# Input weights of a state-space convolution: a product by a weighing matrix, or transposes of a weighed table

## The chip, the cores and the metric

The kernel runs on one core of one Trainium2 chip. The metric is the device time of one execution in microseconds (us): 608.1 as the median of three runs of the kernel before (607.81 to 609.33).

The engines are TensorE (PE, with its weight loads as PEld), VectorE (DVE), ScalarE (ACT), GpSimd (POOL) and SyncE (SP), which only issues transfers. Each works through its own list of instructions in order; semaphores hold an instruction until what it reads is there.

## The reference

```python
# x: (128, 64, 1024) fp32 = batch, head, position; length: (128,) ints
A = -exp(log_A_real) + 1j*A_imag;  dtA = A * exp(log_dt)[:, None]       # 64 heads x 64 states
Cs = C * (exp(dtA) - 1) / A
K  = 2 * einsum('hn,hnl->hl', Cs, exp(dtA[:, :, None] * arange(L))).real
u  = x * (arange(L) < length)                # mask
y  = causal_conv(u, K) + u * D               # the FFT of length 2L is this convolution
y  = y * mask
logits = y @ route_w.T;  w = one_hot(argmax) * max                      # 8 experts
out = x + ((w x (y @ A.T)) @ Bw)             # rank 16 per expert
```

The recurrence is linear, so the convolution of 1024 positions is done in four stretches of Q = 256: inside a stretch by a Toeplitz matrix of K, and from stretch to stretch by the 64 complex states (128 real rows), which are carried with exp(256 dtA).

## The kernel before, in words

A batch of 128 lies on the partitions, and the 64 heads are worked through one after the other, in a software pipeline: step i (line 311, `run_steps`) does some stages for head i, others for heads i-1, i+1, i+2 and i+3. The order on every engine is the order in which the code of that engine is written: a prologue for the first heads by hand, and then its `step` function 64 times. There is no scheduler. Semaphores named for what is done (`grev_done`, `b_mm`, ...) count heads.

For one head the stages are:
- Tables. Every four heads (a `Part`), GpSimd makes step tables (`angle_steps`, L446), ScalarE scales them to turns (L575, L577), VectorE rounds them (`whole_turns`, L867), GpSimd subtracts (`turn_parts`, L457), VectorE finishes and clamps the fraction (L875, L882), ScalarE takes the sine (L583), GpSimd weighs with the magnitudes (`weigh`, L465) and ScalarE mirrors halves (L597). Then per head GpSimd forms `both` (L473) and adds its halves to `Grev` (L483), the powers exp(dtA l) for l = 255..0, states on partitions. `Ghi` and `Glo` (L604, L490) are its split in two parts of lower precision, whose three products give full precision.
- Inputs: how much each of the 256 positions of a stretch gives to each state. TensorE multiplies Grev by the 128x129 matrix `Mx` (L1128, `inputs`): its 128 columns weigh and mix the real and imaginary rows, and the last gives the kernel K itself. ScalarE builds Mx from the constant `twin` and table columns (`m_matrix`, L611, L613). The result `psB` lies in the bank psO0, which the last stage (`up`) also uses. ScalarE and VectorE split it into `Bhi` and `Blo` (L623, L953); the K column goes by `kcol`, a VectorE transpose `krow` (L947) and DRAM, from where it comes back skewed as the Toeplitz table `Traw` (L340, L348), and is split into `Thi` (ScalarE, L629) and `Tlo` (GpSimd, L497).
- Bring (`psS`, L1078): six products of Bhi/Blo and Xhi/Xlo give the states that each stretch brings. ScalarE copies the first (L652), VectorE carries on to the others (`carry`, L936, L940), ScalarE and GpSimd split them (`Shi` L657, `Slo` L512).
- `turn_x`: eight transposes of x (psXe, psXo, L1092); then Xhi (L635), xeven (L640), Xlo (L889 and L505).
- `within` and `from_states` (psYe, psYo, L1078): 9 and 6 products; VectorE masks (`cut`, L966) to Y.
- `project` (psZ, L1103): eight full-precision products give logits and y @ A.T; five short VectorE instructions find the expert and gate (L902 to L924); `turn_wh` transposes (L1162); `whi`, `wlo` (L662, L959); `up` (psO) six products with Bw; VectorE adds x (L975) and the result is stored.

TensorE's order in step i is: bring(i), turn_x(i+1), inputs(i+2), project(i-1), within(i), turn_wh(i-1), from_states(i), up(i-1).

## Time and profile before

| | |
|---|---|
| median of 3 runs | 608.1 us (607.81 to 609.33) |
| profiled execution | 608.38 us, span 606.6 us, granted TensorE clock 0.995 |
| PE busy | 585.7 us, 97% of the span |
| PEld | 532.4 us, 88% |
| DVE | 489.4 us, 81% |
| POOL | 384.1 us, 63% |
| ACT | 315.8 us, 52% |
| chain that ended last | PE 91%, DVE 3%, others 1% or less |

A busy share is a mean over the whole span. Which engine sets the pace is read from the timeline of a stretch: an engine whose instructions follow one another without a hole. In a timeline row the first number is the start, the second the time of all instructions that the row groups; on TensorE a product's duration overlaps the next one's start, so what a group costs is the distance from its start to the next group's start. A full-precision fp32 product is recorded as more than one pass (x4 for two products), a transpose as one.

### The profile page before, as it was taken

Reading aid. Unit: us, or ns where it says so; the run is one execution under the profiler, and the core shown is the slowest. Engines: PE = TensorE matmul, PEld = TensorE weight load, DVE = VectorE, ACT = ScalarE, POOL = GpSimd, SP = SyncE. Lnnn points to the kernel's source line nnn. Section 1 sums busy time; section 2 is a strip of 40 time slices with the busy share of each in tenths; the row PEclk is TensorE's granted clock in tenths of the full one; section 3 lists DMA queues with packets and bytes.
Section 4 is the critical chain, followed back from the end, with each engine's and each line's share of the span. In section 5 each row is a group of like instructions: output and inputs, shape, how many; then the busy total and the mean of one; then the engine's idle time right before and its main releaser. Section 6 shows DMA issues by size and latency. Waiting matters only on the chain.

```text
span 606.6 us, 13395 instructions
## 1 busy us (share of the span) xinstructions
PE 585.7 (97%) x3657; PEld 532.4 (88%) x3657; DVE 489.4 (81%) x1369; ACT 315.8 (52%) x1060; POOL 384.1 (63%) x519
## 2 busy tenths in 40 slices
PE   3879999999999999999999999999999999999996
PEld 3868899999999999999999999999999999999994
DVE  7859878788887878888787888878788887878874
ACT  4747565556446455644645564464556456445420
POOL 4578856666685666667566666756666675675430
PEclk9999999999999999999999999999999999999998
DMA  7114344345334434544443453444345344435521
GB/s 140 54 53 115 130 149 147 103 144 157 112 132 150 147 102 144 158 105 138 150 146 103 145 157 105 138 151 142 107 145 157 101 141 152 134 112 148 157 79 70
DMA packets 37584, 77.65 MB, mean 128 GB/s; under 512 B 12477, under 2 KB 20863, under 8 KB 37511
## 3 DMA queue, kind: packets, MB, share of 16 engines
q1 hardware_dynamic: 28358, 43.76, 28.8%
q10 hardware_dynamic: 9152, 33.03, 13.3%
q8 instruction: 32, 0.52, 0.3%
q14 instruction: 42, 0.34, 0.2%
HBM read 43.16 MB, written 33.62 MB: 127 GB/s over the span
## 4 chain that ended last, share of the span: by engine, by line
PE 91%; DVE 3%; issue 1%; DMA 1%; ACT 1%; ACTq 0%; DVEq 0%; SPq 0%
PE psYo L1078 19%; PE psZ L1103 19%; PE psO L1078 15%; PE psYe L1078 13%; PE psS L1078 11%; PE psO L1128 5%; PE psXo L1092 4%; PE psXe L1092 4%; PE psZ L1162 1%; DVE psS L936 1%; DMA Traw<-kdram 1%; DVE ost L975 0%; DMA kdram<-krow 0%; DVE Sf L940 0%; DVE rho L295 0%
## 5 line engine op out<-in xcount | busy, mean ns | idle before, releaser
L512 POOL TENSOR_TENSOR Slo<-Sf,Shi 128x384 fp32r<-128x384 f32 x64 | 65.2, 1019 | 169.0 <-ACT Shi L657 169.0
L1103 PE MATMUL psZ<-Wt,Y 128*128 128x136 f32 x1024 | 129.2, 279 | 0.0
L936 DVE SCALAR_TENSOR_TENSOR psS<-Sf,tab,psS 64x128 f32<-64x128 f32 x256 | 91.8, 359 | 45.4 <-ACT Sf L652 38.5
L1103 PEld LDWEIGHTS psZ<-Wt,Y 128*128 128x128 f32 x1024 | 123.3, 190 | 0.1
L652 ACT ACTIVATE Sf<-psS 128x128 f32<-128x128 f32 x64 | 17.8, 278 | 198.8 <-PE psS L1078 198.8
L975 DVE TENSOR_TENSOR ost<-psO,xt 128x512 f32<-128x512 f32 x128 | 88.0, 690 | 2.2 <-PE psO L1078 2.0
L505 POOL TENSOR_TENSOR Xlo<-xeven,Xhi 128x512 fp32r<-128x512 f32 x63 | 81.4, 1292 | 0.0
L473 POOL TENSOR_TENSOR both<-coarse,fine 128x512 f32<-128x512 f32 x64 | 68.0, 1063 | 3.4 <-ACT fine L597 3.2
L959 DVE TENSOR_TENSOR wlo<-psZ,whi 128x128 fp32r<-128x128 f32 x64 | 18.7, 292 | 45.1 <-ACT whi L662 45.1
L1078 PE MATMUL psO<-Bw_hi,whi 128*128 128x512 f32 x128 | 50.7, 396 | 3.4 <-ACT whi L662 3.4
L1078 PE MATMUL psO<-Bw_hi,wlo 128*128 128x512 f32 x128 | 51.1, 399 | 0.0
L1078 PE MATMUL psO<-Bw_lo,whi 128*128 128x512 f32 x128 | 50.8, 397 | 0.0
L1078 PE MATMUL psYo<-Xhi,Thi 128*128 128x512 f32 x128 | 50.7, 396 | 0.0
L1078 PE MATMUL psYo<-Xlo,Thi 128*128 128x512 f32 x128 | 50.6, 396 | 0.0
L1078 PE MATMUL psYo<-Xhi,Tlo 128*128 128x512 f32 x128 | 50.3, 393 | 0.0
L483 POOL TENSOR_TENSOR Grev<-both 128x256 f32<-128x256 f32 x64 | 46.8, 732 | 5.0
L490 POOL TENSOR_TENSOR Glo<-Grev,Ghi 128x256 fp32r<-128x256 f32 x64 | 48.1, 751 | 0.7 <-ACT Ghi L604 0.7
L940 DVE SCALAR_TENSOR_TENSOR Sf<-Sf,tab,psS 128x128 f32<-128x128 f32 x128 | 44.5, 348 | 4.5
L497 POOL TENSOR_TENSOR Tlo<-Traw,Thi 128x256 fp32r<-128x256 f32 x64 | 47.1, 735 | 0.2
L657 ACT ACTIVATE Shi<-Sf 128x384 fp32r<-128x384 f32 x64 | 33.7, 526 | 25.5 <-DVE Sf L940 25.5
L1092 PE MATMUL psXe<-ident,xt 128*128 128x128 f32 x256 | 38.8, 274 | 6.9 <-DMA xt<-in_x_dram 6.9
L966 DVE TENSOR_TENSOR Y<-psYe,mask 128x512 f32<-128x512 f32 x64 | 44.1, 689 | 0.8 <-PE psYe L1078 0.8
(200 smaller groups left out, 1526.5 us busy)
## 6 DMA issues: line engine op xcount, KB each, us to landing
xt<-in_x_dram SPq DMA_DIRECT2D x64, 512.0 KB, 4.8
out_dram<-ost ACTq DMA_DIRECT2D x63, 512.0 KB, 5.1
Traw<-kdram SPq DMA_DIRECT2D x64, 128.0 KB, 2.9
kdram<-krow SPq DMA_DIRECT2D x64, 1.0 KB
A_nat<-in_L_ffn_A_dram SPq DMA_DIRECT2D x1, 512.0 KB, 5.0
B_nat<-in_L_ffn_Bw_dram SPq DMA_DIRECT2D x8, 64.0 KB, 3.5
out_dram<-ost SPq DMA_DIRECT2D x2, 256.0 KB, 2.0
lens_i<-in_itok_B_dram SPq DMA_DIRECT2D x1, 64.0 KB, 4.9
```

What stands on the lines that cost most here:

```text
L473: pool.tensor_tensor(both[:, :, :, :], coarse[:, :, h.n, :].rearrange("p t (a b) -> p t a b", b=1).to_broadcast(wide), fine[:, :, h.n, :]. ...
L483: pool.tensor_tensor(Grev[h.s2][:, :], both[:, 0, :, :].rearrange("p a b -> p (a b)"), both[:, 1, :, :].rearrange("p a b -> p (a b)"), ALU ...
L490: pool.tensor_tensor(Glo[h.s4][:, :], Grev[h.s2][:, ::-1], Ghi[h.s4][:, :].bitcast(F32), ALU.subtract).then_inc(glo_done, 1)
L497: pool.tensor_tensor(Tlo[h.s2][:, :, :].rearrange("p a b -> p (a b)"), Traw[h.s2][:, ::-1], Thi[h.s2][:, :, :].rearrange("p a b -> p (a b) ...
L505: pool.tensor_tensor(Xlo[h.s2][:, 0, :], xeven[:, :], Xhi[h.s2][:, 0, :].bitcast(F32), ALU.subtract).then_inc(xlo_even, 1)
L512: pool.tensor_tensor(Slo[h.s2][:, :], Sf[h.s2][:, :], Shi[h.s2][:, :].bitcast(F32), ALU.subtract).then_inc(slo_done, 1)
L936: dve.scalar_tensor_tensor(psS[to, new], Sf[h.s2][fr, old], tab2[fr, BR, h.n:h.n + 1], psS[to, new], ALU.mult, ALU.add).then_inc(brought_d ...
L940: dve.scalar_tensor_tensor(Sf[h.s2][:, new], Sf[h.s2][:, old], col(tab2[:, LR, :], h), psS[:, new], ALU.mult, ALU.add).then_inc(s_carried, 1)
L975: dve.tensor_tensor(ost[h.s2][:, half], psO[j][:, :], xt[h.s4][:, half], ALU.add).then_inc(added, 1)
L1078: mm = pe.matmul(dst, a, b, start=first and i == 0, stop=last and i == n - 1, skip_group_check=True)
L1092: last = pe.transpose(psX[j][:, c * P:(c + 1) * P], xt[h.s4][:, at:at + P], ident[:, :])
L1103: last = pe.matmul(psZ[:, 0:NW], Y[:, j, c, :], Wt[:, 2 * c + j, :], start=(j == 0 and c == 0), stop=(j == 1 and c == NE - 1), skip_group_ ...
```

## The change

The input weights are the same numbers, made in another way. GpSimd and ScalarE weigh the table Grev elementwise while it lies with states on the partitions: `cross_parts` (two copies that swap the halves and scale by table column MB), `same_part` (a copy scaled by MA), `w_table` (the GpSimd sum `Wg`). TensorE then only transposes the two halves of Wg to psB. K comes from the same table: the copies that read psB sum 64 columns each into `kcol` (`accum_out`), and K at position 0, with D added, is computed once for all heads in the prologue (`K0`, which takes the place of CK in pack2), so that kcol has three columns and the two zero rows in DRAM, the matrix `twin` and `Dcol` go. For head 0 VectorE makes Wg (`first_w_table`).

The order changes too: the input transposes stand behind the projection, VectorE does the five gate instructions ahead of x_lo, ScalarE does w_hi ahead of turns and mirror and x_even ahead of Shi, the inputs, krow and Blo of head 2 move from the first step into the prologue, and the magnitudes of heads 8 to 63 (rho16, Exp) are made in two portions of 16 and 40 heads instead of one of 56.

```diff
+        RHO_PARTS = [(0, 2 * FIRST), (2 * FIRST, 4 * FIRST), (6 * FIRST, H - 6 * FIRST)]
 # SyncE
-                sp.dma_start(bass.AP(kdram.tensor, h.s2 * (P + Q), [[G32, P // G32], [P, 2], [1, G32]]),
+                sp.dma_start(bass.AP(kdram.tensor, h.s2 * (P + Q), [[G32, P // G32], [P, 3], [1, G32]]),
...
-            for s in range(2):
-                sp.dma_start(kdram[s:s + 1, Q:Q + P], zeros[:, :]).then_inc(pad_done, 16)
 # GpSimd
+            def w_table(h):
+                need(pool, crossed, h.n * 2 + 2)
+                need(pool, same_done, h.n)
+                need(pool, b_mm, h.n - 1)
+                pool.tensor_tensor(Wg[h.s2][:, :], same[:, :], cross[:, :], ALU.add).then_inc(wg_done, 1)
...
                 if head(3).there and not is_head(head(0), 1):
                     g_table(head(3))
+                if head(2).there:
+                    w_table(head(2))
                 if head(0).there:
                     s_lo(head(0))
 # ScalarE
-            def m_matrix(h):
-                need(act, b_mm, h.n - 1)
-                for j, table in enumerate((M0, M1)):
-                    act.activation(Mx[h.s2][:, j * N:(j + 1) * N], twin[:, j * N:(j + 1) * N], ACT.Copy,
-                                   scale=col(tab2[:, table, :], h)).then_inc(mx_done, 1)
-                act.activation(Mx[h.s2][:, P:P + 1], col(tab2[:, CK, :], h), ACT.Copy).then_inc(mx_done, 1)
+            def cross_parts(h):
+                need(act, grev_done, h.n + 1)
+                need(act, wg_done, h.n)
+                for to, fr in ((slice(0, N), slice(N, P)), (slice(N, P), slice(0, N))):
+                    act.activation(cross[to, :], Grev[h.s2][fr, :], ACT.Copy,
+                                   scale=tab2[fr, MB, h.n:h.n + 1]).then_inc(crossed, 1)
+            def same_part(h):
+                act.activation(same[:, :], Grev[h.s2][:, :], ACT.Copy,
+                               scale=col(tab2[:, MA, :], h)).then_inc(same_done, 1)
             def b_hi(h):
-                act.activation(kcol[h.s2][:, 0, 0:1], psB[:, 0, P:P + 1], ACT.Copy).then_inc(kcol_done, 1)
-                act.activation(kcol[h.s2][:, 1, 0:1], psB[:, 1, P:P + 1], ACT.Identity,
-                               bias=Dcol[:, h.n:h.n + 1]).then_inc(kcol_done, 1)
+                for j in range(2):
+                    act.activation(scrap[:, j, :], psB[:, j, 0:N], ACT.Copy,
+                                   accum_out=kcol[h.s2][:, j, 0:1]).then_inc(kcol_done, 1)
+                act.activation(kcol[h.s2][:, 2, 0:1], col(tab2[:, K0, :], h), ACT.Copy).then_inc(kcol_done, 1)
...
             def step(head):
+                if head(2).there:
+                    cross_parts(head(2))
+                    same_part(head(2))
                 if head(-2).there:
                     store(head(-2))
                 if head(0).there:
                     first_state(head(0))
-                if head(3).there:
-                    m_matrix(head(3))
 # VectorE
+            def first_w_table(h):
+                need(dve, crossed, h.n * 2 + 2)
+                dve.scalar_tensor_tensor(Wg[h.s2][:, :], Grev[h.s2][:, :], col(tab2[:, MA, :], h), cross[:, :],
+                                         ALU.mult, ALU.add).then_inc(wg_done, 1)
...
+            link(dve.reduce_sum(ksum[:, :], CK[:, 0, :], axis=AX.X))
+            TT(pack2[:, K0, 0, 0:1], ksum[:, :], D_nat[:, :], ALU.add).then_inc(pack2_done, 1)
 # TensorE
-                need(pe, mx_done, h.n * 3 + 3)
-                need(pe, grev_done, h.n + 1)
+                need(pe, wg_done, h.n + 1)
                 for j in range(2):
-                    last = pe.matmul(psB[:, j, :], Grev[h.s2][:, j * P:(j + 1) * P],
-                                     Mx[h.s2][:, :], start=True, stop=True, skip_group_check=True)
+                    last = pe.transpose(psB[:, j, :], Wg[h.s2][:, j * P:(j + 1) * P], ident[:, :])
...
-                if is_head(head(0), 1):
-                    inputs(head(1))
-                elif head(2).there:
-                    inputs(head(2))
                 if head(-1).there:
                     project(head(-1))
-                if is_head(head(0), 1):
+                if head(2).there:
                     inputs(head(2))
```

On TensorE, in a step of the middle of the program, the end of bring and the start of within stood so before:

```order
L1078 MATMUL psS<-Xhi,Blo 128x384
L1092 MATMUL psXe<-ident,xt 128x128 x4
L1092 MATMUL psXo<-ident,xt 128x128 x4
L1128 MATMUL psO<-Mx,Grev 128x129 x2
L1103 MATMUL psZ<-Wt,Y 128x136 x8
L1078 MATMUL psYe<-Xhi,Thi 128x512
```

and stand so now, in the same step:

```order
L1101 MATMUL psS<-Xhi,Blo 128x384
L1115 MATMUL psXe<-ident,xt 128x128 x4
L1115 MATMUL psXo<-ident,xt 128x128 x4
L1126 MATMUL psZ<-Wt,Y 128x136 x8
L1150 MATMUL psO<-ident,Wg 128x128 x2
L1101 MATMUL psYe<-Xhi,Thi 128x512
```

The two products of 129 columns became two transposes and moved behind the eight products of the projection.

On GpSimd, where a step's extra work (`angle_steps` and `weigh`) comes, it stood so before, from the end of one step to the Slo of the next:

```order
L490 TENSOR_TENSOR Glo<-Grev,Ghi 128x256
L446 TENSOR_TENSOR step_h<-tab,grid 128x64
L446 TENSOR_TENSOR step_t<-tab,grid 128x64
L446 TENSOR_TENSOR step_l<-tab,grid 128x64
L465 TENSOR_TENSOR coarse<-wave,mag 128x64
L465 TENSOR_TENSOR fine<-wave,mag 128x64 x2
L473 TENSOR_TENSOR both<-coarse,fine 128x512
L483 TENSOR_TENSOR Grev<-both 128x256
L512 TENSOR_TENSOR Slo<-Sf,Shi 128x384
```

and now:

```order
L488 TENSOR_TENSOR Glo<-Grev,Ghi 128x256
L435 TENSOR_TENSOR step_h<-tab,grid 128x64
L435 TENSOR_TENSOR step_t<-tab,grid 128x64
L435 TENSOR_TENSOR step_l<-tab,grid 128x64
L454 TENSOR_TENSOR coarse<-wave,mag 128x64
L454 TENSOR_TENSOR fine<-wave,mag 128x64 x2
L462 TENSOR_TENSOR both<-coarse,fine 128x512
L474 TENSOR_TENSOR Grev<-both 128x256
L482 TENSOR_TENSOR Wg<-same,cross 128x256
L510 TENSOR_TENSOR Slo<-Sf,Shi 128x384
```

One instruction came in: the sum Wg, behind all of the step's table work and ahead of Slo.

On ScalarE the start of a step stood so before:

```order
L652 ACTIVATE Sf<-psS 128x128
L611 ACTIVATE Mx<-twin,tab 128x64 x2
L613 ACTIVATE Mx<-tab 128x1
L635 ACTIVATE Xhi<-psXe 128x512
L635 ACTIVATE Xhi<-psXo 128x512
L619 ACTIVATE kcol<-psO 128x1
L620 ACTIVATE kcol<-psO,Dcol 128x1
L623 ACTIVATE Bhi<-psO 128x256
L657 ACTIVATE Shi<-Sf 128x384
L640 ACTIVATE xeven<-psXe 128x512
```

and now:

```order
L617 ACTIVATE cross<-Grev,tab 64x256 x2
L622 ACTIVATE same<-Grev,tab 128x256
L657 DMA out_dram<-ost 128x1024
L664 ACTIVATE Sf<-psS 128x128
L647 ACTIVATE Xhi<-psXe 128x512
L647 ACTIVATE Xhi<-psXo 128x512
L652 ACTIVATE xeven<-psXe 128x512
L669 ACTIVATE Shi<-Sf 128x384
L631 ACTIVATE scrap,kcol<-psO 128x64 x2
L633 ACTIVATE kcol<-tab 128x1
L635 ACTIVATE Bhi<-psO 128x256
```

The weighing copies stand ahead of the first state, and everything that reads psB stands behind Shi.

## Rows read from the trace of the kernel before

**Rows 1.** Timeline, TensorE, head 31: start us, us, engine line operation.
```profile
304.86 0.34 PE L1078 MATMUL psS<-Xhi,Bhi 128*128 128x384 f32 x1
...
305.91 0.60 PE L1092 MATMUL psXe<-ident,xt 128*128 128x128 f32 x4
...
306.34 0.60 PE L1092 MATMUL psXo<-ident,xt 128*128 128x128 f32 x4
...
306.78 0.61 PE L1128 MATMUL psO<-Mx,Grev 128*128 128x129 f32 x4
...
307.22 2.02 PE L1103 MATMUL psZ<-Wt,Y 128*128 128x136 f32 x16
...
308.99 0.48 PE L1078 MATMUL psYe<-Xhi,Thi 128*128 128x512 f32 x1
...
313.72 0.34 PE L1078 MATMUL psS<-Xhi,Bhi 128*128 128x384 f32 x1
```

**Rows 2.** Costliest groups: busy us, mean ns, then idle before, and its releaser.
```profile
L652 ACT ACTIVATE Sf<-psS 128x128 f32<-128x128 f32 x64 | 17.8, 278 | 198.8 <-PE psS L1078 198.8
...
L959 DVE TENSOR_TENSOR wlo<-psZ,whi 128x128 fp32r<-128x128 f32 x64 | 18.7, 292 | 45.1 <-ACT whi L662 45.1
```

**Rows 3.** Timeline, GpSimd, heads 31 and 32, with the extra work.
```profile
309.60 1.01 POOL L512 TENSOR_TENSOR Slo<-Sf,Shi 128x384 fp32r<-128x384 f32 x1 [3.45 <-ACT Shi L657]
...
314.81 1.05 POOL L473 TENSOR_TENSOR both<-coarse,fine 128x512 f32<-128x512 f32 x1
315.94 0.73 POOL L483 TENSOR_TENSOR Grev<-both 128x256 f32<-128x256 f32 x1
```

**Rows 4.** Groups by form, ScalarE: a copy of 256 columns and one of 1.
```profile
L604 ACT ACTIVATE Ghi<-Grev 128x256 fp32r<-128x256 f32 x64 | 26.1, 408 | 3.7 <-POOL Grev L483 3.7
...
L619 ACT ACTIVATE kcol<-psO 128x1 f32<-128x1 f32 x64 | 11.1, 174 | 2.4 <-PE psO L1128 2.4
```

**Rows 5.** Timeline, VectorE and GpSimd, end of step 33 and step 34.
```profile
332.24 0.22 DVE L867 TENSOR_SCALAR whole<-turns_t 128x128 f32<-128x128 f32 x1
...
332.53 0.45 POOL L457 TENSOR_TENSOR frac<-whole,turns_h 128x128 f32<-128x128 f32 x1 [1.65 <-DVE whole L867]
332.94 1.05 POOL L473 TENSOR_TENSOR both<-coarse,fine 128x512 f32<-128x512 f32 x1
334.07 0.73 POOL L483 TENSOR_TENSOR Grev<-both 128x256 f32<-128x256 f32 x1
```

**Rows 6.** Timeline, VectorE and TensorE, startup (steps 1 to 3).
```profile
38.25 0.38 DVE L953 TENSOR_TENSOR Blo<-psO,Bhi 128x256 fp32r<-128x256 f32 x1
...
38.69 0.71 PE L1128 MATMUL psO<-Mx,Grev 128*128 128x129 f32 x4 [1.07 <-DVE Blo L953]
...
45.54 0.47 PE L1078 MATMUL psO<-Bw_hi,whi 128*128 128x512 f32 x1 [2.63 <-ACT whi L662]
...
47.01 0.34 PE L1078 MATMUL psS<-Xhi,Bhi 128*128 128x384 f32 x1
...
56.92 0.33 PE L1078 MATMUL psS<-Xhi,Bhi 128*128 128x384 f32 x1
```

**Rows 7.** Timeline, VectorE and GpSimd, ends of step 30 and of step 2.
```profile
305.42 0.73 POOL L483 TENSOR_TENSOR Grev<-both 128x256 f32<-128x256 f32 x1
305.67 0.70 DVE L875 SCALAR_TENSOR_TENSOR frac<-step_l,frac 128x64 f32<-128x64 f32 x2
...
306.40 0.23 DVE L882 TENSOR_SCALAR fraction<-frac 128x128 f32<-128x128 f32 x1
...
306.66 0.75 DVE L936 SCALAR_TENSOR_TENSOR psS<-Sf,tab,psS 64x128 f32<-64x128 f32 x2
...
58.04 0.73 POOL L483 TENSOR_TENSOR Grev<-both 128x256 f32<-128x256 f32 x1
...
58.22 0.64 DVE L882 TENSOR_SCALAR fraction<-frac 128x128 f32<-128x128 f32 x1
```

**Rows 8.** Busy time by stretch, end of the run (PE, PEld, DVE, ACT, POOL; PEclk, DMA share, GB/s).
```profile
600.00:604.00 4.00, 2.59 (x6) 1.57 (x6) 1.68 (x3) 0.15 (x1) 0.00 (x0) 0.62 0.13 50
```

More of the change, by code:

```diff
@@ L77, in conv_ffn_kernel @@
         V, VH, VL, RHO = range(4)
-        LR, M0, M1, BR, CK = range(5)
+        LR, MA, MB, BR, K0 = range(5)
         pack1 = sb("pack1", [H, 4, 2, N])
@@ L134, in conv_ffn_kernel @@
         Glo = [sb(f"Glo{s}", [P, Q], F32R) for s in range(4)]
-        Mx = [sb(f"Mx{s}", [P, P + 1]) for s in range(2)]
-        kcol = [sb(f"kcol{s}", [P, 2, G32]) for s in range(2)]
-        krow = [sb(f"krow{s}", [P, 2, G32]) for s in range(2)]
+        same = sb("same", [P, Q])
+        cross = sb("cross", [P, Q])
+        Wg = [sb(f"Wg{s}", [P, Q]) for s in range(2)]
+        scrap = sb("scrap", [P, 2, N])
+        kcol = [sb(f"kcol{s}", [P, 3, G32]) for s in range(2)]
+        krow = [sb(f"krow{s}", [P, 3, G32]) for s in range(2)]
         Bhi = [sb(f"Bhi{s}", [P, 2, P], F32R) for s in range(2)]
@@ L462, in weigh @@
                 need(pool, wave_done, part.k + 1)
-                pool.wait_ge(mag_done, 4 if part.k > 1 else 2)
+                pool.wait_ge(mag_done, 2 * sum(part.start >= start for start, _ in RHO_PARTS))
                 for table, half, size in ((coarse, 0, COARSE), (fine, 0, FINE), (fine, 1, FINE)):
@@ L528, in step @@
                 if is_head(head(0), 1):
-                    weigh(parts[1])
-                    g_lo(head(1))
-                    g_table(head(3))
                     g_lo(head(2))
@@ L534, in step @@
                     t_lo(head(1))
+                if is_head(head(0), 1):
+                    g_table(head(3))
                 if head(3).there:
@@ L549, in _ @@
             turn_parts(parts[1])
+            w_table(first[1])
+            g_table(first[2])
             s_lo(first[0])
@@ L552, in _ @@
             x_lo(first[1])
-            g_table(first[2])
+            w_table(first[2])
             g_lo(first[1])
+            g_table(first[3])
+            weigh(parts[1])
             t_lo(first[1])
-            g_table(first[3])
+            g_lo(first[2])
             angle_steps(parts[2])
@@ L693, in step @@
                     g_hi(head(2))
+                if part_at(head(7)):
+                    turns(part_at(head(7)))
+                if head(3).there:
                     g_hi(head(3))
+                if part_at(head(4)):
+                    mirror(part_at(head(4)))
                 if is_head(head(0), 2):
-                    act.wait_ge(rho_done, 2)
-                    magnitudes(slice(2 * FIRST, H))
+                    magnitudes(1)
+                if is_head(head(0), 6):
+                    magnitudes(2)
                 if part_at(head(5)):
@@ L980, in step @@
                     carry(head(0))
-                if head(1).there:
-                    x_lo(head(1))
-                if is_head(head(0), 1):
-                    turn_k(head(1))
-                    b_lo(head(1))
                 if head(-1).there:
@@ L991, in step @@
                     gated(head(-1))
+                if head(1).there:
+                    x_lo(head(1))
                 if head(2).there:
@@ L1004, in step @@
                     exponents(dve, *RHO_PARTS[1])
+                if is_head(head(0), 4):
+                    exponents(dve, *RHO_PARTS[2])
                 if part_at(head(7)):
@@ L1048, in _ @@
             x_lo_even(first[0])
+            first_w_table(first[0])
             masks(0)
@@ L1066, in _ @@
                 cut(first[0], j)
+            turn_k(first[2])
+            b_lo(first[2])
             run_steps(step)
@@ L1211, in keep_busy @@
                     pe.matmul(bank_[:, 0:P], ident[:, :], ident[:, :], start=True, stop=True, skip_group_check=True)
-            first = [Head(n) for n in range(2)]
-            pe.wait_ge(consts, 9)
+            first = [Head(n) for n in range(3)]
+            pe.wait_ge(consts, 5)
             turn_x(first[0], 0)
@@ L1259, in _ @@
             within(first[0], 1)
+            inputs(first[2])
             run_steps(step)
```

102 lines of the change are left out of this document (44 added, 58 removed).

## The prediction

> **What bounds the kernel now.** I read the timeline of one whole head first, engine by engine, then the costliest groups, then the startup. TensorE's row of head 31 [rows 1] has no hole: the state product at 304.86 (psS) comes back at 313.72, 8.86 us later, and each group starts where the one before stops issuing. From head 3 (56.92, [rows 6]) to head 31 that is 247.94 us for 28 heads, 8.855 each, so nothing but TensorE's issue sets the time of the long middle. The other engines wait for it: ScalarE idles 198.8 us in all ahead of its first state copy, VectorE 45.1 us ahead of wlo [rows 2]. GpSimd [rows 3] starts each head's row of work at Slo, 4.74 us after the state product (309.60), and in a head that also prepares the next four heads' tables its Grev ends only at 316.67, well into the next head. In before nobody needs that Grev for a whole further head. This is the point on which the change turns.
>
> **The change part by part.**
>
> *The input products.* Before, two full-precision products per head (4 passes, psO<-Mx,Grev) take 306.78 to 307.22, 0.44 us of issue. Four transposes of the same shape take 305.91 to 306.34, 0.43 us, so one takes 0.11 [rows 1]. After, there are two transposes: 0.22. TensorE saves 0.22 us a head, 0.88 in four, if nothing is late: 8.64 a head.
>
> *The table Wg that they transpose.* It now needs, per head, three ScalarE copies of 256 columns (two of them on half the partitions) and one GpSimd add of 128x256. ScalarE: the like copy Ghi takes 0.41 [rows 4]; three are 1.22, in exchange for Mx and two narrow copies, and they stand ahead of the first state where ScalarE waits 3 us a head [rows 2]: nothing, while that cover lasts. The two copies that now sum 64 columns as well are a kind that the trace does not show; bounds 0.17 and 0.41 each (the one-column copy that they replace, and the copy of 256 columns; [rows 4]). They stand behind Shi; what waits for them is Blo, which has until wlo, and VectorE idles 0.7 a head there [rows 2]. I take 0.3 each, between the ends, and no loss; at 0.41 each the cover is just used up, +1 us over the run at most, and at 0.17 nothing changes. VectorE: the transpose of kcol grows from 64 to 96 columns and stands, with x_lo, behind the gates; both lie ahead of wlo in the same wait: nothing. The gates come 0.6 earlier, which no one misses.
>
> *GpSimd's add, and when it is due.* Its length is that of Grev, 0.73, and it starts 0.70 after Grev starts, since GpSimd begins an instruction 0.04 before the end of one that it does not wait for (both at 332.94, frac to 332.98, [rows 5]). It is due where the input transposes now stand, behind the projection: the within products start at 308.99, less the 0.44 that left the row, 308.55, which is 3.69 after the head's state product [rows 1]. A result reaches TensorE about 0.08 after it ends: at 38.69 a product started 0.06 after the end of the Blo that it waited for [rows 6], and I add 0.02 for its first weight load, which then lies beside nothing. GpSimd's queue puts w_table(i+2) behind g_table(i+3), so in a head with extra work the add waits for all of that, though its own inputs are long ready. Three kinds of head:
> - plain: both starts right behind Glo, some 1.6 us ahead of where it stands in the head with extra work [rows 3], and Wg is ready 1.3 us early. No stall.
> - every fourth, heads 4 to 52 (13 of them), with three step tables and three weighings ahead [rows 3]: Grev starts at 315.94, Wg at 316.64, ends 317.37, reaches TensorE at 317.45, 12.59 after 304.86. Due at 8.64 + 3.69 = 12.33. Stall 0.26.
> - two heads later, 6 to 54 (13): GpSimd waits for VectorE's rounding (whole ends 332.46), then frac, both, Grev at 334.07 [rows 5]; Wg 334.77 to 335.50, there at 335.58. This head's state product is at 331.43 (304.86 and three times 8.855), so it comes at 4.15 where 3.69 is due. Stall 0.46. The rounding hangs on TensorE's up products by way of the adds, and does not come earlier when the row is shorter.
>
> In each of these heads TensorE has nothing else to issue, and with no slack anywhere in its row the stall is lost whole.
>
> *A second effect of the longer GpSimd row.* After head 6, 10, ... VectorE does frac and clamp just ahead of the next carry. The pair frac takes 0.70 [rows 7] and ends 0.22 after GpSimd's Grev ends (306.15), and at 58.22 clamp takes 0.64 instead of 0.23 and ends 0.09 after Grev does: such instructions of VectorE wait for GpSimd's running one. After the change GpSimd will be in Wg when clamp comes, and the carry, which now starts 0.03 behind clamp, slips by 0.07 (clamp alone waits) to 0.42 (frac too). That goes by Shi and Slo into the next head's GpSimd row, so into the 0.26. I take 0.12, near the case in which clamp alone waits, since in the rows frac gets in between two GpSimd instructions: stall 0.38.
>
> The Trainium skill says the same of the place (GPSIMD Engine Reference, 1. Specifications): the SBUF interfaces are shared, and GpSimd contends with VectorE instructions that run in a two-port mode or have two SBUF inputs. Clamp (one SBUF input) and frac (two) behave so here; by that rule the carry's own instructions, which read PSUM, are free. It does not say who goes first at a boundary, which is the difference between 0.07 and 0.42.
>
> *The sum in the middle.* A group of four: 0.46 + 0.38 = 0.84 lost against 0.88 saved. 13 groups: -0.5 us. Seven heads outside the groups (3, and 56 to 61) have no extra work ahead of their add: -1.5.
>
> *Startup.* Longer ahead of the first state: a reduction and an add for K0 (about +0.27), the second b_high now ahead of the crosses (+0.47), crosses, a VectorE product in place of Mx, and the summing copies: state product 0 about 0.9 later. Gained in step 1: the inputs of head 2 and its krow come before the steps, so Thi(2) is no longer what up(0) waits for (TensorE sat 2.63 at 45.54, [rows 6]); I put the state product of head 2 at 45.5 against 47.01. Lost again in step 2: GpSimd does Glo(4) (held by ScalarE's Ghi(4)), frac and g_table(5) ahead of w_table(4), so inputs(4) stall about 3.1 us. State product 3 at 57.3 against 56.92: +0.4, bounds -2 and +3 (none or twice of the two stalls changes by so much). The exponents of 40 heads and their table load (1.28) now fall in heads 4 and 6, where little cover is left: +0.5, bounds 0 and 1.5. The D load, the zero rows and the twin table that go are off the path.
>
> Sum: 606.6 - 0.5 - 1.5 + 0.4 + 0.5 = 605.5 of span. The profiled execution took 608.38 in all, 1.8 outside its span; 607.3. It lies 0.3 above the median of the runs, 608.1; I take 607.3.
>
> **The rivals.**
> - *GpSimd is in time*: the stalls are 0.2 shorter each than read, or GpSimd's row starts earlier. At no stall at all 13 x 0.84 = 10.9 less, 596.4; at 0.2 less each, 5.2 less, 602.1. For it: two of four heads have over a microsecond to spare, and each stall is a difference of two numbers near 12. Against it: both come from one chain of durations that vary by 0.02 in the trace.
> - *The carry slips* (slower): frac waits too, 0.42, the second stall becomes 0.68, and Slo comes about 0.1 late for the state products of the heads after it: 0.46 + 0.68 + 0.1 = 1.24 against 0.88, 13 groups +4.7, less 1.5, plus 0.9 and up to 1 more of startup: 610.7 of span, 612.5. It decides once the carry slips more than about 0.2: then a group costs more than it saves. For it: [rows 7]. Against it: in the stalled head GpSimd's row starts 0.46 earlier against TensorE's, so Wg may be nearly over when frac comes.
> - *Startup decides*: the stalls at inputs(3) and inputs(4) go away or double, -2 or +3 alone: 605 or 610.
> - *The clock falls*: at the end of the run, where TensorE works 2.59 of 4 us, the granted clock is 0.62 of full [rows 8], so part of the stretch is at the lower level of 1.2 GHz. If the startup stall of 3.1 us does that, some products there take twice their time: +2, 609.3. Against it: 2.63 us of waiting at 45.54 did not.
>  The Trainium skill (TensorE: Matmul & The Clock Gate, Part 4: PE-mode transpose) holds that transposes do not count as work for the clock. Nine of a head's issue slots are transposes now, and two more take the place of full products; the middle of before ran at the upper level with nine, so I give that rule 1 in 50. By it the time would be far above my range.
>
> **How the numbers follow.** Forecast (gain given back on GpSimd) 0.38; GpSimd in time 0.27, of which the full gain 0.07; carry slips 0.18; startup decides 0.13; clock 0.04. About 0.3% (1.8 us) is what a measurement tells from no change: faster is below 606.3, slower above 609.9. The forecast's own range is 605 to 609.5, and a quarter of it lies below 606.3. Faster: 0.27 + 0.25 x 0.38 + a third of startup, 0.41. Slower: 0.18 + 0.04 + some of startup, 0.23. Same: 0.36. Range 602 to 611.5: the partial gain below, most of the slipping carry above; the full gain and the doubled loss are left out.
>
> **What would show it.** In the profile after: two psO<-Wg passes a head, 0.22 of issue; TensorE idle before them, 0.46 in heads 6, 10, ... and about 0.4 in heads 8, 12, ..., put down to GpSimd's Wg, and no other wait in the middle; four heads in about 35.4 us as before; GpSimd busy some 47 us more, ScalarE idle ahead of Sf down by some 70; the state product of head 3 near 57. Wrong it is if the stalls are on other heads or every head (ScalarE's summing copies, then wlo), if a period of four is under 35.0 or over 35.8, or if the inputs save other than 0.22.

## The result, and the profile after

The changed kernel takes 615.42 us (median of 4 runs, 615.03 to 615.87); the kernel before took 608.47 beside it (607.81 to 609.33). The ratio is 1.0117, with a 95% interval of 1.0101 to 1.0133: it is 7 us slower. The prediction was 607.3, its range 602 to 611.5: wrong, on the slower side and outside the range. The profiled execution has a span of 613.4 us.

The page shows first that TensorE's own work did shrink, and that the end no longer hangs on it alone (busy times, then the chain of work that ended last):

```profile
PE 581.1 (95%) x3529; PEld 522.5 (85%) x3529; DVE 500.5 (82%) x1374; ACT 405.3 (66%) x1255; POOL 427.3 (70%) x576
issue 37%; POOL 26%; PE 24%; ACT 6%; DVE 2%; POOLq 1%; ACTq 0%; DVEq 0%
```

GpSimd's row and the issues that wait for it are now in the chain. The waits of the changed kernel (engine, line, releaser: us in total, times, longest) name the place:

```profile
ACT Sf L664 <- PE psS L1101: 61.4, 59, 3.5
DVE wlo L977 <- ACT whi L674: 30.8, 47, 1.9
PEld psO L1150 <- issue: 15.7, 28, 3.1
PE psO L1150 <- POOL Wg L482: 10.8, 28, 2.9
```

ScalarE had 198.8 us of idle time ahead of its first state copy [rows 2] and has 61.4, which is 137 less where the forecast had some 70; VectorE's 45.1 ahead of wlo fell to 30.8. GpSimd is busy for 43.2 us more, where 47 was forecast. TensorE waits for Wg 28 times: twice for each of the 13 groups of four heads, as was forecast, and twice in the startup. TensorE's rows of heads 30 to 33 (timeline; start, duration, then idle time in brackets) answer to [rows 1]:

```profile
302.50 0.34 PE L1101 MATMUL psS<-Xhi,Bhi 128*128 128x384 f32 x1
306.71 0.41 PE L1150 MATMUL psO<-ident,Wg 128*128 128x128 f32 x2 [0.27 <-POOL Wg L482]
...
320.27 0.34 PE L1101 MATMUL psS<-Xhi,Bhi 128*128 128x384 f32 x1
322.21 2.02 PE L1126 MATMUL psZ<-Wt,Y 128*128 128x136 f32 x16
324.53 0.41 PE L1150 MATMUL psO<-ident,Wg 128*128 128x128 f32 x2 [0.30 <-POOL Wg L482]
```

The state products of heads 30 to 34 start at 302.50, 311.58, 320.27, 329.43 and 338.09. The distances are 9.08, 8.69, 9.16 and 8.66: 35.59 for a group of four, where before had four times 8.855, 35.42. In the last heads, where no add is late, the distance is 8.61 to 8.65; the forecast had 8.64. So the 0.22 us are there in every head, and they are given back in two heads of four.

Why the second of the two stalls is the longer one stands in VectorE's and GpSimd's rows just ahead of the carry of head 31 (timeline):

```profile
312.39 1.02 DVE L887 SCALAR_TENSOR_TENSOR frac<-step_l,frac 128x64 f32<-128x64 f32 x2
313.45 0.23 DVE L894 TENSOR_SCALAR fraction<-frac 128x128 f32<-128x128 f32 x1
313.70 0.75 DVE L948 SCALAR_TENSOR_TENSOR psS<-Sf,tab,psS 64x128 f32<-64x128 f32 x2
```
```profile
311.90 0.74 POOL L474 TENSOR_TENSOR Grev<-both 128x256 f32<-128x256 f32 x1
312.59 0.74 POOL L482 TENSOR_TENSOR Wg<-same,cross 128x256 f32<-128x256 f32 x1
320.24 0.30 POOL L435 TENSOR_TENSOR step_h<-tab,grid 128x64 f32<-128x64 f32 x1
321.83 1.06 POOL L462 TENSOR_TENSOR both<-coarse,fine 128x512 f32<-128x512 f32 x1
322.98 0.73 POOL L474 TENSOR_TENSOR Grev<-both 128x256 f32<-128x256 f32 x1
323.66 0.72 POOL L482 TENSOR_TENSOR Wg<-same,cross 128x256 f32<-128x256 f32 x1
```

The pair frac takes 1.02 instead of 0.70 [rows 7] and ends 0.08 after GpSimd's Wg (313.41 against 313.33). The second instruction of the pair has waited for Wg; the clamp, for which the forecast had the wait, takes its plain 0.23. And Wg stands last in GpSimd's row of step 32, 3.4 us behind step_h.

The larger part of the loss is the startup. The state products of heads 0 to 3 start at 26.44, 38.55, 48.39 and 61.62, where they started at 24.35, 33.23, 47.01 and 56.92 [rows 6]. Here the forecast for head 3 was 57.3. TensorE's rows ahead of it (timeline), and then three stretches by windows (window, length, busy us and instructions of PE, PEld, DVE, ACT and POOL, then PEclk, the granted clock as a share of full, DMA share, GB/s):

```profile
34.84 0.77 PE L1101 MATMUL psYe<-Xhi,Thi 128*128 128x512 f32 x1 [0.88 <-POOL Tlo L495]
35.40 0.63 PE L1101 MATMUL psYe<-Xlo,Thi 128*128 128x512 f32 x1
55.28 0.66 PE L1150 MATMUL psO<-ident,Wg 128*128 128x128 f32 x2 [2.95 <-POOL Wg L482]
55.59 0.78 PE L1101 MATMUL psYe<-Xhi,Thi 128*128 128x512 f32 x1
...
59.06 0.27 PE L1183 MATMUL psZ<-ident,wh 128*128 128x128 f32 x1
```
```profile
34.80:38.20 3.40, 3.36 (x9) 2.68 (x10) 0.69 (x1) 0.00 (x0) 3.40 (x4) 0.54 0.13 30
50.00:54.00 4.00, 2.33 (x21) 2.13 (x19) 1.78 (x5) 2.93 (x7) 3.32 (x6) 1.00 0.77 269
55.30:58.30 3.00, 3.00 (x9) 2.42 (x10) 2.35 (x9) 1.62 (x8) 2.16 (x2) 0.50 0.00 0
```

From 55.30 to 58.30 TensorE runs at 0.50 of full, its lower level of 1.2 GHz, after the wait of 2.95 us; products of 128x512 follow each other at 0.43 instead of 0.23.

Summed up from these dates, against the span of before (606.6): startup to head 3 +4.7, heads 3 to 56 +2.85, heads 56 to 63 -1.3, behind the last state product +0.5. That is 6.8.

### The profile page after: what moved, and what is told of

Read it like the earlier page. It is cut to its first block, busy times and chain, and to the rows that moved or that the text cites. A ratio compares the mean times of both kernels' runs of the same rounds, so it can differ in the third digit from the quotient of the medians.

```text
span 613.4 us, 13517 instructions
## 1 busy us (share of the span) xinstructions
PE 581.1 (95%) x3529; PEld 522.5 (85%) x3529; DVE 500.5 (82%) x1374; ACT 405.3 (66%) x1255; POOL 427.3 (70%) x576
## 4 chain that ended last, share of the span: by engine, by line
issue 37%; POOL 26%; PE 24%; ACT 6%; DVE 2%; POOLq 1%; ACTq 0%; DVEq 0%
PE psYo L1101 7%; POOL both L462 6%; POOL Wg L482 6%; PE psYe L1101 5%; PE psZ L1126 3%; POOL Tlo L495 3%; POOL Glo L488 3%; PE psO L1101 3%; PE psS L1101 2%; ACT cross L617 2%; PE psO L1150 2%; POOL fine L454 1%; POOLq L312 1%; POOL Xlo L503 1%; ACT same L622 1%
## 5 line engine op out<-in xcount | busy, mean ns | idle before, releaser
L669 ACT ACTIVATE Shi<-Sf 128x384 fp32r<-128x384 f32 x64 | 33.6, 525 | 57.3 <-DVE Sf L952 57.3
L617 ACT ACTIVATE cross<-Grev,tab 64x256 f32<-64x256 f32 x128 | 64.8, 506 | 2.8
L664 ACT ACTIVATE Sf<-psS 128x128 f32<-128x128 f32 x64 | 17.7, 276 | 61.4 <-PE psS L1101 61.4
L674 ACT ACTIVATE whi<-psZ 128x128 fp32r<-128x128 f32 x64 | 17.7, 277 | 54.6 <-PE psZ L1183 54.6
L482 POOL TENSOR_TENSOR Wg<-same,cross 128x256 f32<-128x256 f32 x63 | 46.4, 737 | 5.5 <-ACT cross L617 2.8
```

The source lines that it names most:

```text
L482: pool.tensor_tensor(Wg[h.s2][:, :], same[:, :], cross[:, :], ALU.add).then_inc(wg_done, 1)
L617: act.activation(cross[to, :], Grev[h.s2][fr, :], ACT.Copy, scale=tab2[fr, MB, h.n:h.n + 1]).then_inc(crossed, 1)
```

## The experiments

Each ratio is against the kernel before, timed beside it; its median was 607.43 for the early add, the clock and the two single edits in the startup, 608.54 for the guard, TensorE's part and all together, and 608.79 for the last three kernels. The theory was: the middle is GpSimd's order, the startup is order and clock. The rivals were ScalarE's longer row in the middle, and a startup loss that is plain extra work.

**The early add.** One line of GpSimd's step, moved:

```diff
+                if head(2).there:
+                    w_table(head(2))
                 if part_at(head(6)):
                     turn_parts(part_at(head(6)))
                 ...
-                if head(2).there:
-                    w_table(head(2))
```

> The changed kernel with one line of GpSimd's step moved: the add that makes Wg for the head after the next stands directly behind angle_steps, ahead of the step tables, the weighings and the g_table. Theory (the middle's loss is GpSimd's order alone): the waits of TensorE's input transposes go from heads 6, 10, ... and 8, 12, ...; a group of four heads takes 34.6 us instead of 35.59, all heads 8.64 to 8.66; step 2 of the startup stalls less too (2.95 before its inputs now). Time 615.4 less 13 x 0.93 less 0 to 2.5: 601 to 604. Rival (ScalarE's longer row is late next, its copies for Wg and the summing copies): the waits move to ScalarE's work, a group keeps 35.2 or more, 610 or more. Rival (GpSimd's tables are now late by one add more, so the x_lo and carries slip): the clamp still waits, 606 to 609.

Measured: 608.15 us, ratio 1.0011 (0.9998 to 1.0024). It gives back nearly the whole loss, and is no faster than before. Of what it gives back 5.1 us lie between heads 3 and 56, and 1.4 in the startup (state product 3 at 60.22; the wait ahead of the inputs of head 4 is 2.19 instead of 2.95). The two stalls are gone, and TensorE waits for Wg twice instead of 28 times: heads follow at 8.65, 8.61 and 8.65, and then one of 9.31 to 9.34 comes in each group of four. The group takes 35.25, 0.65 more than the first theory's 34.6, and the third expectation, the one on the clamp, came true. VectorE and GpSimd ahead of the carry of head 31 (timeline):

```profile
307.23 1.23 DVE L887 SCALAR_TENSOR_TENSOR frac<-step_l,frac 128x64 f32<-128x64 f32 x2
308.49 0.64 DVE L894 TENSOR_SCALAR fraction<-frac 128x128 f32<-128x128 f32 x1
309.17 0.75 DVE L948 SCALAR_TENSOR_TENSOR psS<-Sf,tab,psS 64x128 f32<-64x128 f32 x2
```
```profile
306.49 0.74 POOL L482 TENSOR_TENSOR Wg<-same,cross 128x256 f32<-128x256 f32 x1 [0.39 <-issue]
307.19 1.05 POOL L462 TENSOR_TENSOR both<-coarse,fine 128x512 f32<-128x512 f32 x1
308.32 0.73 POOL L474 TENSOR_TENSOR Grev<-both 128x256 f32<-128x256 f32 x1
```

frac ends 0.22 after both ends, the clamp 0.08 after Grev ends: each waits for the running GpSimd instruction, and the carry starts 1.06 after its Sf is there (308.11). Its own instructions keep their 0.75 for two: over all heads none of them takes under 0.351 or over 0.368.

**The guard.** To the early add comes one wait: GpSimd's both of that head waits for the clamp.

```diff
                 need(pool, grev_done, h.n)
+                if h.n > 6 and part_at(Head(h.n + 2)):
+                    need(pool, frac_done, part_at(Head(h.n + 2)).k + 1)
```

> The kernel with the early add (e1_early_w) and one wait more: in the head in which VectorE makes the fractions of four heads (frac, clamp), GpSimd's both waits until the clamp is done; GpSimd has 3 us of idle time behind it there. Theory (what is left of the middle's loss, 0.67 us in each group of four, is VectorE's frac 1.23 and clamp 0.64 held by GpSimd's running Wg, both and Grev, which makes the next carry 1.0 late and by it the gates and the first state's products): frac and clamp take 0.5 and 0.23 again behind Wg, the carry starts within 0.2 of its Sf, a group takes 34.6 to 34.8, time 608.2 less 13 x 0.55 = 601. Rival (the stall comes from the gates behind a late projection, or the wait only moves Grev and with it cross and the next Wg): a group stays at 35.3, time 607 to 609.

Measured: 601.41 us, ratio 0.9886 (0.9865 to 0.9906). From head 10 on all heads but the last take 8.64 or 8.65, 34.6 for four. The same places (timeline, VectorE and GpSimd):

```profile
304.45 0.35 DVE L889 SCALAR_TENSOR_TENSOR frac<-step_l,frac 128x64 f32<-128x64 f32 x2
304.83 0.23 DVE L896 TENSOR_SCALAR fraction<-frac 128x128 f32<-128x128 f32 x1
305.36 0.75 DVE L950 SCALAR_TENSOR_TENSOR psS<-Sf,tab,psS 64x128 f32<-64x128 f32 x2 [0.30 <-ACT Sf L666]
```
```profile
305.23 1.06 POOL L464 TENSOR_TENSOR both<-coarse,fine 128x512 f32<-128x512 f32 x1 [0.77 <-DVE fraction L896]
306.36 0.73 POOL L476 TENSOR_TENSOR Grev<-both 128x256 f32<-128x256 f32 x1
308.30 1.02 POOL L512 TENSOR_TENSOR Slo<-Sf,Shi 128x384 fp32r<-128x384 f32 x1 [1.21 <-ACT Shi L671]
```

An added wait made the kernel some 7 us faster (the ratios differ by 1.25%): GpSimd gives 0.77 us that it has (1.21 of idle time is still left ahead of Slo), VectorE gets 1.3 back (0.58 for the three instructions instead of 1.87), and TensorE the 0.65 of each group that it had been waiting. With both edits the middle's mechanism is shown from both sides.

**TensorE's part alone.** The kernel before, with the two products turned into transposes of Grev; weighing and the kernel's constant are left out of the computation, the K column takes numbers from the transposes.

```diff
-                    last = pe.matmul(psB[:, j, :], Grev[h.s2][:, j * P:(j + 1) * P],
-                                     Mx[h.s2][:, :], start=True, stop=True, skip_group_check=True)
+                    last = pe.transpose(psB[:, j, 0:P], Grev[h.s2][:, j * P:(j + 1) * P], ident[:, :])
```

> The kernel before with one edit: TensorE's two full-precision input products are two transposes of Grev; the weighing and the kernel's constant are left out of the result. Everything else (order, ScalarE's Mx, GpSimd) stays. It measures what TensorE's part alone is worth. Theory (TensorE's row is the bound and has 0.22 us less of it): 8.64 a head and no wait in the middle, 608.1 less 61 x 0.215 = 595. Rival (another engine is right behind TensorE in the kernel before too, and takes part of the gain): 8.70 to 8.80 a head, 598 to 604.

Measured: 600.71 us, ratio 0.9878 (0.9859 to 0.9896). The rival holds: a group takes 34.9 (8.76, 8.86, 8.69 and 8.60 from head 31 on, 8.73 in the mean), between 34.6 and 35.42. Two engines are right behind TensorE in the old order: once the gates stand behind a late carry (frac takes 0.91 ahead of it), and a head later ScalarE's whi stands behind the mirror copies, and wlo, which the last stage needs too, behind whi (it ends at 316.35). TensorE's weight loads and ScalarE's rows (timeline):

```profile
306.45 0.14 PEld L1161 LDWEIGHTS psZ<-ident,wh 128*128 128x128 f32 x1 [0.34 <-DVE wh L924]
316.42 0.19 PEld L1078 LDWEIGHTS psO<-Bw_hi,whi 128*128 128x128 f32 x1 [0.27 <-issue]
```
```profile
315.33 0.54 ACT L597 ACTIVATE fine<-fine 64x64 f32<-64x64 f32 x2
315.77 0.25 ACT L662 ACTIVATE whi<-psZ 128x128 fp32r<-128x128 f32 x1
```

The guarded kernel takes 34.6 a group, 0.3 less, 4 us over 13 groups. It has the gates ahead of x_lo and whi ahead of the mirror copies, which is where these rows wait; that the 4 us come from these two moves is argued, since no run makes them alone.

**The clock.** The changed kernel with more idle-time products on TensorE, in the startup only:

```diff
-            keep_busy(psY[0], 8)
+            keep_busy(psY[0], 12)
             from_states(first[0])
+            keep_busy(psZ, 5)
             within(first[0], 0)
...
+                if is_head(head(0), 2):
+                    for _ in range(12):
+                        pe.matmul(psY[0][:, 0:P], ident[:, :], ident[:, :], start=True, stop=True,
+                                  skip_group_check=True)
```

> The changed kernel with more idle-time products on TensorE in the startup alone (12 instead of 8 ahead of the first state product, 5 more ahead of the first within products, 12 ahead of the inputs of head 4): they do nothing for the output and run where TensorE waits. Theory (about 3 us of the startup's loss is TensorE's lower clock after its waits): the products at 34.8 to 38.0 and 55.3 to 58.3 go at 0.175 or 0.23 instead of 0.43, state product 3 comes at 58.5 to 59.5 instead of 61.6, time about 612.5. Rival (the clock is down for another reason, or others are late next and keep the dates): state product 3 within 0.5 of 61.6, time 615 to 616.

Measured: 613.82 us, ratio 1.0097 (1.0075 to 1.012), 1.2 us less by the ratios, whose intervals overlap. State product 3 comes at 60.39 instead of 61.62, between the theory and the rival. TensorE's row and the granted clock there (timeline; windows):

```profile
55.51 0.41 PE L1150 MATMUL psO<-ident,Wg 128*128 128x128 f32 x2 [0.79 <-POOL Wg L482]
55.67 0.48 PE L1101 MATMUL psYe<-Xhi,Thi 128*128 128x512 f32 x1
57.84 0.27 PE L1183 MATMUL psZ<-ident,wh 128*128 128x128 f32 x1
```
```profile
55.50:58.00 2.50, 2.49 (x13) 2.06 (x14) 2.36 (x9) 1.60 (x8) 1.64 (x2) 1.00 0.00 0
```

Wg is no earlier than in the changed kernel, but the within products take 2.17 us instead of 3.47 (59.06 less 55.59): 1.3 us, which is the clock. At 34.8 too the products ran at the upper level, and state product 1 came 1.16 earlier; of this only 0.31 is left at product 2, since the wait for Wg of head 3 grew from 0.52 to 1.78. The theory's size, 3 us, was the sum of both; half of it was hidden. At 34.8 the filling was not what kept the clock up, at least not alone: the early-add and the guarded kernel have the changed kernel's prologue, without more filling, and their granted clock was 1.00 there (state product 1 at 37.80 and 37.49).

**Two edits to single causes in the startup.** The sum for K0 behind the four table products; and the first Thi ahead of the copies for head 2:

```diff
-            link(dve.reduce_sum(ksum[:, :], CK[:, 0, :], axis=AX.X))
             for table, half, a, b, op in (...
                 ...
+            link(dve.reduce_sum(ksum[:, :], CK[:, 0, :], axis=AX.X))
```
```diff
+            t_hi(first[0])
             cross_parts(first[2])
             same_part(first[2])
-            t_hi(first[0])
```

> The changed kernel with the sum of the kernel's real parts (for K0) taken behind the four products of the tables instead of ahead of them. Theory (the reduction pushed the four into GpSimd's running instruction, 1.50 us instead of 0.62): the four end about 1.0 earlier, the transposed tables come near 20.8 instead of 21.66, the first state product at about 25.5 instead of 26.44; time 614.4 to 615. Rival (the four are held by the shared port wherever they stand, or K0 stands on the path anyway): first state product within 0.2 of 26.44, time as the changed kernel's, 615.4.

> The changed kernel with ScalarE's first turned copy (Thi of head 0) ahead of the three copies for the Wg of head 2. Theory (Thi(0) stood behind 1.57 us of copies whose data came later): within(0) starts 0.9 to 1.5 earlier than 34.84, TensorE's clock stays up there, state product 1 at 36.5 to 37.5 instead of 38.55; what it gives at state product 3 is less, 0 to 1.5, since Wg of head 2 comes later by 0.4; time 614 to 615.4. Rival (the wait only moves to the inputs of head 2, which stand behind): state product 3 at 61.6 and the time 615.4 to 616.

Measured: 616.04 (ratio 1.0124, 1.0091 to 1.0158) and 613.13 (1.0081, 1.0052 to 1.0111). In the first the four products take 0.62 instead of 1.50, as expected; yet the small add behind them now takes 0.76, so it has only passed GpSimd's instruction on, and the first state product comes 0.4 earlier, at 26.04, not 0.9. Even the 0.4 can't be put down to the sum: the guarded kernel, whose sum stands where it stood, has 26.08. In the second the state products 1 and 2 come at 36.24 and 46.62, 2.3 and 1.8 earlier. Against the early-add and the guarded kernel, which kept the upper clock at 34.8, it is 1.3 to 1.6 at product 1 and 1.6 to 1.7 at product 2: that much is the order. Neither profile keeps it: head 3 stands at 62.96 and 61.68, since the inputs of head 4 wait longer, 3.45 us, and the lower clock then lasts longer. But each profile is of the slowest of its four executions (616.65 and 615.61); what the faster ones kept (down to 613.1 and 612.3) isn't shown. TensorE's row and windows of the kernel with the sum moved:

```profile
55.56 0.66 PE L1150 MATMUL psO<-ident,Wg 128*128 128x128 f32 x2 [3.45 <-POOL Wg L482]
```
```profile
55.50:61.00 5.50, 5.44 (x15) 4.49 (x16) 2.73 (x10) 2.29 (x11) 2.97 (x4) 0.50 0.05 11
```

**All together.** The add first in GpSimd's step, the guard, the sum and Thi moved, 9 instead of 2 idle-time products ahead of the first inputs, and in steps 1 and 2 the table of head 4 first:

```diff
                 if is_head(head(0), 1):
-                    g_lo(head(2))
+                    g_table(head(3))
                 if head(1).there:
                     t_lo(head(1))
...
+                if is_head(head(0), 1, 2):
+                    g_lo(head(2))
...
+                if is_head(head(0), 2):
+                    first_state(head(0))
                 if head(2).there:
                     cross_parts(head(2))
                     same_part(head(2))
```

> All that the runs so far point to, in one kernel: the add first in GpSimd's step, the wait of both for the clamp, the sum behind the table products, Thi(0) ahead of the copies for head 2, 9 instead of 2 idle-time products ahead of the first inputs, and in steps 1 and 2 the table of head 4 (g_table, cross, same) ahead of Glo(3), Tlo(2) and Ghi(4), with the first state copy of head 2 ahead of them. Theory (the startup's loss is the order around the Wg of heads 2 to 4): state product 1 at 35.5 to 36.5, product 2 at 45 to 46, product 3 at 54.5 to 56 instead of 61.6; with the middle of the guarded kernel 594 to 597. Rival (TensorE's clock or ScalarE's length, not the order, sets product 3): product 3 at 58 or later, 598 to 601.

Measured: 596.7 us, ratio 0.9812 (0.9791 to 0.9832); state products 1 to 3 at 36.01, 46.39 and 56.21, the second and third 0.4 and 0.2 later than the theory's bounds. The inputs of head 4 wait 0.18 instead of 2.95. Two kernels take one part out of it.

> The combined kernel without the new order of steps 1 and 2 (the table of head 4 stands behind Glo(3), Tlo(2) and Ghi(4) again). Theory (that order makes the 2.2 to 2.95 us wait ahead of the inputs of head 4): the wait is back, 2.2 us, state product 3 at 58 to 60 instead of 56.2, time 599 to 600. Rival (with everything ahead of it earlier, the wait is already short): product 3 within 1 of 56.2, time 597.

Without the order of steps 1 and 2: 599.35 us, ratio 0.9858 (0.983 to 0.9885). The wait of 2.19 us is back and product 3 comes at 57.11, 0.9 later. As products 0 to 2 come 1.2 earlier here, the step from product 2 to 3 is 11.90 instead of 9.82: the theory holds, at 2.1 us.

> The combined kernel with 2 idle-time products ahead of the first inputs, as the changed kernel has, instead of 9. It tells what the lower clock after TensorE's wait at 22 to 24 us costs. Theory: the first state products go at 0.32 instead of 0.175 a product and the transposes after them too, 1.5 us; but they start 0.9 earlier (26.0), so state product 1 comes 0 to 0.8 later than 36.0 and the time is 596.5 to 597.5. Rival (the wait for GpSimd and the states hides it all): product 1 within 0.2 of 36.0, or earlier by up to 0.9, time 595.8 to 596.7.

With 2 products instead of 9: 598.3 us, ratio 0.9834 (0.9813 to 0.9855), product 1 at 36.06 and product 3 at 56.26. The dates fit both expectations, the time lies above both. The two profiles show no gain from the nine, but the kernel without the order of steps 1 and 2, which has the same nine in the same place, shows why. TensorE's row in it and in the combined kernel (timeline), and the windows from 22 to 24 us of both, in the same order:

```profile
21.48 2.17 PE L1230 MATMUL psO<-ident 128*128 128x128 f32 x18
```
```profile
21.42 3.67 PE L1234 MATMUL psO<-ident 128*128 128x128 f32 x18
```
```profile
22.00:24.00 2.00, 1.83 (x17) 1.64 (x17) 0.72 (x3) 1.64 (x4) 1.59 (x3) 1.00 0.00 0
```
```profile
22.00:24.00 2.00, 2.00 (x11) 2.00 (x11) 0.78 (x3) 1.58 (x4) 1.59 (x3) 0.50 0.00 0
```

The same 18 matmuls (nine products, two passes each) take 2.17 us at the full clock in one profiled execution and 3.67 at half of it in the other, with the same products on TensorE ahead of them; in the first, product 1 comes at 34.83, 1.2 earlier. The clock in the startup is partly a matter of the execution. So the theory and its rival can't be told apart by one profile, and the difference of the timed runs, 0.2%, is within what the intervals allow. The combined kernel's own executions fit this: the profiled one took 597.98, the other three 596.63 to 596.73. It may also explain the wide runs of the two single edits (613.1 to 616.65 and 612.3 to 615.61, where the changed kernel has 615.03 to 615.87). Both are argued from the profiles and not shown.

**The last version.** Where the combined kernel still waited: Wg of head 3 ahead of Glo(2), the adds of heads 6 and 10 behind the step tables and weighings, the state copies of heads 1, 3 and 7 ahead of the cross copies, the wait for the clamp in step 3 too, 6 idle-time products:

```diff
             t_lo(first[1])
+            w_table(first[3])
             g_lo(first[2])
...
-                if is_head(head(0), 2):
+                if is_head(head(0), 1, 2, 3, 7):
                     first_state(head(0))
```

> The combined kernel with its last waits aimed at: the Wg of head 3 ahead of Glo(2) and the step tables, the adds of heads 6 and 10 behind the step tables and weighings (their copies come late there, after a table load), the first state copies of heads 1, 3 and 7 ahead of the cross copies, 6 idle-time products instead of 9, and the wait for the clamp in step 3 too. Theory (GpSimd's and ScalarE's order around late copies, 1.48 us ahead of inputs(3), 0.77 in head 4, 0.74 and 0.38 in heads 7 and 8): state product 2 at 45.2, product 3 at 55.0, heads 4, 7 and 8 at 8.65 to 8.9, time 593.5 to 595. Rival (state product 3 hangs on the chain state copy, carry, gates, not on Wg): product 3 at 56, time 595.5 to 597.

Measured: 594.59 us, ratio 0.9775 (0.9752 to 0.9799), 2.25% faster than the kernel before. The page (busy, and the chain) and the window from 100 to 500 us:

```profile
PE 570.6 (96%) x3537; PEld 518.4 (88%) x3537; DVE 493.2 (83%) x1374; ACT 402.4 (68%) x1255; POOL 428.9 (72%) x576
PE 90%; DVE 2%; issue 2%; POOL 2%; ACT 1%; ACTq 0%; POOLq 0%; DVEq 0%
```
```profile
100.00:500.00 400.00, 400.00 (x2507) 366.01 (x2506) 337.76 (x924) 282.27 (x893) 307.98 (x405) 1.00 0.46 138
```

TensorE is busy for 400.00 of 400 us. State products 1 to 3 come at 34.91, 44.23 and 54.06. Products 2 and 3 are 1 us better than expected, and heads 4 and 8 take 8.66, as expected; but head 7 still takes 9.42, and head 3 now takes 9.40 where it had 8.64.

## Why the prediction was wrong, point by point

The mechanism of the middle was right. The step that failed is the size of two terms of the sum: the startup, taken at +0.4 (state product 3 at 57.3) and measured at +4.7, and the middle, where the slip of the carry was taken at 0.12 and the 53 heads from 3 to 56 measured 3.0 more than the sum had. With 0.5 behind the last state product these make the 7.9 us by which the span, 613.4, exceeds the sum's 605.5.

- *TensorE saves 0.22 us a head.* Right: 8.64 to 8.65 a head wherever nothing is late, and from head 10 on in the guarded kernel.
- *The places of the stalls.* Right: the inputs in the steps of heads 6, 10, ... and 8, 12, ..., released by GpSimd's Wg. Moving the add took both away.
- *Their size.* Heads 6, 10, ...: 0.46 forecast, 0.44 measured (9.08 less 8.64). Heads 8, 12, ...: 0.38 forecast, 0.52 measured (9.16 less 8.64). What failed in it is the slip of the carry, taken at 0.12 near the case in which the clamp alone waits. The rows show that frac waits instead: its pair is 0.32 longer, the clamp no longer than before. The two other heads also take 0.02 and 0.05 more than 8.64. A group loses 1.03 instead of 0.84, and at 35.59 against 35.42 it gained nothing and lost 0.17: with the table load and the exponents, the 53 heads from 3 to 56 cost 3.0 us more than the sum had. This is the rival *the carry slips*, at some half of its surplus per group.
- *Startup: state product 3 at 57.3.* Measured 61.62; the largest error, 4.3 us, and outside the bounds of -2 and +3 by itself. By the dates 2.9 of it stand at product 2, put at 45.5 and measured at 48.39, and 1.4 in the step from there to product 3. Four things stood in it. Product 0 was put 0.9 later and came 2.09 later. The rows show two longer pieces ahead of it: behind the reduction VectorE's next four products ran into a GpSimd instruction (1.50 instead of 0.62), and the cross copies take 506 ns each, where the row of Ghi had given 408. With the sum moved it came at most 0.4 earlier, so the rest of the 2.09 stays open. Thi of head 0 stood behind three copies for head 2, which the argument had not priced: with Thi first, product 2 came 1.6 to 1.8 earlier. The stall at inputs(4) was seen at 3.1 and was 2.95; that term was right. And its consequence was put at 1 in 25: after it TensorE ran at 0.50 of full from 55.3 to 58.3, 1.3 us.
- *The clock falls.* The rival was right for the startup, though its argument against (2.63 us of waiting at 45.54 did not do it, [rows 6]) was a true row. Waits of 2.95 and 3.45 were followed by the lower level each time; one of 0.88 at 34.84 as well, with TensorE idle for 1.50 shortly ahead of it, but not in the early-add and the guarded kernel, where the same wait of 0.88 had 0.99 and 0.81 of idle time ahead of it; one of 2.19 was not in the early-add kernel (0.41 for the transposes behind it), and was in the guarded kernel (0.66). The length of one wait does not decide it, and a row without a fall does not exclude one. By the Trainium skill (TensorE: Matmul & The Clock Gate, Part 4: PE-mode transpose) transposes do not count as work for the clock; in the last version eleven issue slots of a head are transposes and the granted clock is 1.00 over 400 us, so transposes among products did not bring it down here.
- *ScalarE's cover and the exponents.* Right as to the cover in the middle, where no wait of TensorE is put down to ScalarE: the summing copies took 0.21 and their read-out 0.20, spaced 0.20 a pair, below the 0.3 assumed. The table loads cost more than the 0.5 taken, one long head (9.38, head 7) where heads at the same place of a group take 8.69.
- *Within the Trainium skill's rule on shared interfaces* (GPSIMD Engine Reference, 1. Specifications): frac and clamp waited, the carry's instructions, which read PSUM, never did (0.35 to 0.37 each in all heads). The trace agrees, and adds what the forecast lacked: VectorE waits to the end of each running GpSimd instruction, again for the next one, so in the early-add kernel a close row of three held three instructions for 1.3 us in all.

What stays open: the rest of product 0's delay, the 0.5 us behind the last state product (18.72 before, 19.26 after, 18.8 in the guarded kernel), why heads 3 and 7 take 9.4 in the last version, and what lets TensorE's clock fall in one execution of the startup and not in another.

## What to carry to other kernels

When an engine that nobody waited for becomes a supplier, price its place in the queue, not its length: the add's 0.73 us were free, its place behind the table work of the step cost 0.44 and 0.52 us in two heads of four, and one moved line gave both back. Look then for the collision that the faster row uncovers: a wait added to an engine with time to spare can be worth more than a wait removed. Price a startup as its own chain, step by step with each engine's queue, and for a stall on TensorE like those of 2.95 and 3.45 us here price the products behind it at the lower clock too.

## What the runs showed of the hardware

- A pair of small VectorE products (0.35 together where nothing runs) took 0.70, 1.02 or 1.23 according to how GpSimd's instructions of 0.73 and 1.05 stood; in each of these rows it ended 0.08 or 0.22 after one of theirs.
- ScalarE's copy of 64x256 across partition halves took 506 ns, and same, of 128x256 with the same kind of scale, 0.51; a plain copy of 128x256 took 0.41.
- An activation with a sum beside it is two entries: 0.21 for the copy of 128x64, 0.20 for the read-out, overlapped so that a pair costs 0.20.
- TensorE's clock fell to 0.50 of full behind a startup wait of 2.19 us in one kernel and not in two others, and TensorE ran 18 like matmuls at either level in two executions; once down it stayed there for up to 5.5 us of busy work (55.50 to 61.00).
